# Masks from the first landing on, 14 pieces of block 1 ahead of the first fill, and layer 0 by pairs: a three-pass graph attention kernel on one core

## The reference

```python
def gat(h, mask, u, v, values):            # one pass
    e = leaky_relu(u[:, None] + v[None, :], 0.2)
    att = softmax(where(mask, e, -9e15), axis=1)
    return elu(att @ values)
# layer 0: values = entity_embs, then x = layernorm(x + elu(att @ entity_embs + x))
# layers 1, 2: h = 0.2 * x + 0.8 * gat(h, ...);  concat(x, h1, h2) @ mlp_w + mlp_b, residual, layernorm
```

## Time and profile before

| | us |
|---|---|
| median of 3 runs | 3445.28 (3441.72 to 3446.64) |
| the profiled execution | 3447.01 |
| its span in the trace | 3445.2 |

### The profile page before, as it was taken

How to read it: one execution, slowest core, us unless ns; L and a number is a source line. 1 busy time by engine, 2 the same in 40 slices (tenths; PEclk the granted TensorE clock), 3 DMA queues, 4 the chain that set the end, 5 groups by cost and what they waited for, 6 DMA issues and landing times. The chain is left out here.

```text
span 3445.2 us, 56585 instructions
## 1 busy us (share of the span) xinstructions
PE 3096.8 (90%) x21977; PEld 1071.2 (31%) x21977; DVE 2865.5 (83%) x5292; ACT 2274.0 (66%) x3934; POOL 280.9 (8%) x330
## 2 busy tenths in 40 slices
PE   1479999999999999699999999997999999999998
PEld 0123333333333333233333333332333333333333
DVE  5468888888888876699999999997888788888886
ACT  0247776666766767477777777784666666666665
POOL 0000000000000000000000000001112112211211
PEclk9989999999999999899999999998999999999999
DMA  8999999999999981221312222214667766766764
GB/s 242 287 346 342 342 338 338 335 341 333 342 341 332 342 259 55 86 86 64 112 71 105 79 96 87 88 62 135 166 158 166 188 155 161 178 167 163 170 150 80
DMA packets 441759, 679.29 MB, mean 197 GB/s; under 512 B 297474, under 2 KB 318082, under 8 KB 416914
## 3 DMA queue, kind: packets, MB, share of 16 engines
q1 hardware_dynamic: 409458, 564.40, 51.2%
q0 software_dynamic: 32032, 111.27, 16.2%
HBM read 430.10 MB, written 77.69 MB: 147 GB/s over the span
## 5 line engine op out<-in xcount | busy, mean ns | idle before, releaser
L1235 DVE SCALAR_TENSOR_TENSOR eps<-ua,v8col,cb 128x512 f32<-128x512 f32 x2800 | 1963.9, 753 | 294.5 <-ACT prob L630 218.4
L630 ACT ACTIVATE prob<-eps,v2col 128x512 f32<-128x512 f32 x2392 | 1526.2, 689 | 599.1 <-PE eps L810 588.9
L851 PE MATMUL acc<-prob,feat 128*64 128x512 f32 x4784 | 1216.5, 605 | 6.4 <-ACT acc_s L638 6.4
L810 PE MATMUL eps<-nt,nbig 128*64 128x512 fp8e4 (+2 forms) x6642 | 997.5, 385 | 150.7 <-DVE eps L1235 146.5
L810 PEld LDWEIGHTS eps<-nt,nbig 128*64 128x64 bf16 (+2 forms) x6642 | 327.7, 103 | 1032.0 <-DVE eps L1235 687.7
L851 PEld LDWEIGHTS acc<-prob,feat 128*64 128x64 f32 x4784 | 305.9, 137 | 381.7 <-issue 208.0
L1065 DVE TENSOR_SCALAR mi<-stage 128x1024 uint8<-128x1024 int32 x512 | 351.7, 688 | 66.4 <-DMA stage<-in_adj_dram 66.0
L630 ACT ACTIVATE mi<-eps,v2col 128x512 f32<-128x512 f32 x344 | 219.5, 687 | 102.0 <-PE eps L810 100.3
L630 ACT ACTIVATE stage<-eps,v2col 128x512 f32<-128x512 f32 x336 | 214.6, 687 | 95.1 <-PE eps L810 93.4
L860 PE MATMUL den<-prob,ones 128*32 128x512 f32 x2048 | 275.5, 610 | 0.0
L1074 DVE TENSOR_SCALAR edges<-nt 128x2048 int32<-128x2048 int32 x192 | 234.0, 1219 | 29.7 <-PE misc L821 15.2
(11 more groups left out here) (175 smaller groups left out, 1810.4 us busy)
## 6 DMA issues: line engine op xcount, KB each, us to landing
stage<-in_adj_dram SPq DMA_DIRECT2D x512, 512.0 KB, 6.8
nt<-nt_d SPq DMA_DIRECT2D x128, 1024.0 KB, 6.1
nt_d<-nt SPq DMA_DIRECT2D x64, 1024.0 KB, 7.1
prob<-prob POOLq DMA_DIRECT2D x64, 512.0 KB, 5.8
mi<-mi POOLq DMA_DIRECT2D x64, 512.0 KB, 6.4
stage<-stage POOLq DMA_DIRECT2D x64, 512.0 KB, 6.6
ub<-u_d SPq DMA_DIRECT2D x48, 256.0 KB, 5.2
xy_d<-xin POOLq DMA_DIRECT2D x32, 256.0 KB, 3.3
```

The source lines that it names most:

```text
L630: nc.scalar.activation(weights(l, b, j), eps[:, j % ES, :], ACT.Exp, bias=v2col[:, j:j + 1]).then_inc(s_p, 1)
L810: mm = nc.tensor.matmul(et[c:c + cols, :], nbig[:, c:c + cols], edge, start=False, stop=True, skip_group_check=True, tile_position=(0, c))
L851: mm = nc.tensor.matmul(acc[h:h + C, :], feat[:, l % 2, j, 0:C], weights(l, b, j), start=(k == 0), stop=(k == NT // 2 - 1))
L1235: dv.scalar_tensor_tensor(eps[:, j % ES, :], ua[:, par, :], v8col[:, j:j + 1], cb[:, par, :], ALU.add, ALU.max).then_inc(s_fill, 1)
```

## The change

- SP issues the first adjacency loads (now four) ahead of the weights, and x after unit 7. VectorE makes masks 0 to 3 first of all.
- `node_products` is split into the product and the sum (`node_sums`), and masks stand between these, `bounds`, `levels`, the edges and the head of block 0.
- `PRO`, the number of units ahead of the first fill, goes from 32 to 46, so block 0's loop makes 38 units instead of 52. `units_at` of the other blocks is as before.
- Four stage buffers instead of five (`SS`), six mask buffers instead of eight (`MR`).
- Layer 0 issues its mains by pairs after every second mask, two pairs behind, and its denominators two quads at a time, after the step t with t % 8 = 3; masks are 64 columns wide.
- `prob` has 12 slots instead of 8. In layer 2 the ring of 24 slots is the same size, with `mi` and `stage` holding 4 and 8 of them instead of 8 and 8.

```diff
-MR = 8
-PRO = UNITS
+MR = 6
+PRO = UNITS + 14
+X_AT = 7
+UB_AT = UNITS + 3
-SS = 5
+SS = 4
-GROUP = (QUAD, 2, 2)
-LAG = (1, 2, 2)
+PAIRLAG = 2
-TS = 2 * QUAD
-SLOTS = (TS, TS, 3 * TS)
+LAST_RING = 6
+TS = 3 * QUAD
-MASK_COLS = (32, 64, 64)
+HALF = 64
@@ sync
+            for h in range(SS):
+                adj_load(h)
             sp.wait_ge(s_zero, 4)
...
-            for h in range(SS):
-                adj_load(h)
-            sp.dma_start(feat[:, 1, :, 0:C], x.rearrange("(t p) c -> p t c", p=P)).then_inc(s_x0, 16)
             for h in range(PRO):
                 unit(h)
+                if h == X_AT:
+                    sp.dma_start(feat[:, 1, :, 0:C], x.rearrange("(t p) c -> p t c", p=P)).then_inc(s_x0, 16)
+                if h == UB_AT:
+                    sp.wait_ge(s_ust, 16)
+                    ub_load(0, 0, 0)
@@ scalar, probs
-                if l < 2 and j % GROUP[l] == 0 and not (l == 0 and b == 0 and j < TS):
-                    act.wait_ge(s_main, summed(l, b, j - TS + GROUP[l] - 1))
+                if l < 2 and tile(l, b, j) >= TS and j % 2 == 0:
+
+                    old, i = divmod(tile(l, b, j) - TS, NT)
+                    ol, ob = divmod(old, NB)
+                    if ol == 1:
+                        act.wait_ge(s_main, pairs(ol, ob, i // 2 + 1))
+                    else:
+                        act.wait_ge(s_den, dens(ol, ob, i // DEN + 1))
@@ tensor
-                n = GROUP[l]
-                first = j // n * n - 1
+                first = j // 2 * 2 - 1
...
-                return P if any(first <= t < first + n for t in whole) else MASK_COLS[l]
+                return P if any(first <= t < first + 2 for t in whole) else HALF
...
+            def two_quads(l, b, g):
+                denominators(l, b, 2 * g)
+                denominators(l, b, 2 * g + 1).then_inc(s_den, 1)
...
-                        if t % GROUP[l] == GROUP[l] - 1:
-                            k = t // GROUP[l] - LAG[l]
+                        if t % 2 == 1:
+                            k = t // 2 - PAIRLAG
                             if k >= 0:
-                                sums(l, b, k)
+                                main(l, b, k).then_inc(s_main, 1)
                             elif tail:
-                                sums(l, b - 1, NT // GROUP[l] + k)
+                                main(l, b - 1, NT // 2 + k).then_inc(s_main, 1)
...
+                        if l == 0 and t % DEN == DLAG:
+                            g = t // DEN - 1
+                            if g >= 0:
+                                two_quads(l, b, g)
+                            elif tail:
+                                two_quads(l, b - 1, NT // DEN + g)
@@ vector
+            for h in range(SS):
+                make_mask(h)
             dve.wait_ge(s_w, 16 * 14)
...
+                    masks(SS, 8)
                     dve.wait_ge(s_w0e, 1)
                     dve.wait_ge(s_feat0, 16)
                     node_products(0)
+                    masks(8, 10)
+                    node_sums(0)
+                    masks(10, 12)
                     bounds(0)
-                    for h in range(SS):
-                        make_mask(h)
+                    masks(12, 14)
                     levels(0)
+                    masks(14, 18)
                     dve.wait_ge(s_x0, 16)
                     node_products(1)
+                    masks(18, 20)
+                    node_sums(1)
                     dv.memset(feat[:, 1, :, C - 1:C], 1.0).then_inc(s_one, 1)
-                    for h in range(SS, PRO):
-                        make_mask(h)
-                        if h in (MU + 6, 2 * MU + 6):
-                            make_edges(0, 0, h // MU - 1)
+                    masks(20, 24)
+                    make_edges(0, 0, 0)
+                    masks(24, 28)
+                    make_edges(0, 0, 1)
+                    masks(28, UNITS + 6)
+                    make_edges(0, 0, 2)
+                    masks(UNITS + 6, UNITS + 9)
+                    make_edges(0, 0, 3)
+                    masks(UNITS + 9, UNITS + 12)
+                    head(0, 0, 0, 0)
+                    head(0, 0, 0, 1)
+                    head(0, 0, 0, 2)
+                    masks(UNITS + 12, PRO)
+                    add_u(0, 0, 0)
```

More of the change, by code:

```diff
@@ L318, in places @@
         def places(b, j):
-            q, o = divmod((b * NT + j) % SLOTS[2], TS)
-            return (prob[:, :, :], more, rest)[q], o
+            n = (b * NT + j) // QUAD % LAST_RING
+            buf = (prob[:, :, :], prob[:, :, :], prob[:, :, :], as_probs(mi[:, 0:QUAD, :]),
+                   as_probs(stage[:, :, :]), as_probs(stage[:, :, :]))[n]
+            return buf, (0, QUAD, 2 * QUAD, 0, 0, QUAD)[n] + j % QUAD
         def weights(l, b, j):
             if l < 2:
-                return prob[:, j % SLOTS[l], :]
+                return prob[:, tile(l, b, j) % TS, :]
             buf, o = places(b, j)
@@ L347, in den_blocks, with pairs, dens @@
             return b if l == 0 else (l - 1) * NB + b
[L349 to L357, removed]
+        def pairs(l, b, n):
+            return (l * NB + b) * (NT // 2) + n
+        def dens(l, b, n):
+            return den_blocks(l, b) * (NT // DEN) + n
         def started(l, b, j, on_act):
@@ L491, in body @@
                     if l == 0:
+                        ub_at = min((t for t in units_at(b) if t >= 10), default=NT)
                         for t, hs_ in sorted(units_at(b).items()):
-                            if t >= 10 and t < 12:
+                            if t == ub_at:
                                 ub_load(l, b + 1, 1 - par)
@@ L498, in body @@
                             store(NB * MV - 1)
-                        if head and not any(t in (10, 11) for t in units_at(b)):
+                        if head and ub_at == NT:
                             ub_load(l, b + 1, 1 - par)
@@ L633, in sums_out @@
             def sums_out(l, b, par):
[L634 to L637, removed]
+                act.wait_ge(s_main, pairs(l, b, NT // 2))
                 nc.scalar.activation(acc_s[:, :], acc[:, :], ACT.Copy).then_inc(s_acce, 1)
             def denominators_out(l, b):
[L641 to L644, removed]
+                act.wait_ge(s_den, dens(l, b, NT // DEN))
                 nc.scalar.activation(den_s[:, :], den[:, :], ACT.Copy).then_inc(s_dene, 1)
@@ L862, in denominators @@
                 return mm
[L864 to L871, removed]
             def eight_probs(b, g):
@@ L1013, in _ @@
                 blocks(body)
[L1014 to L1019, removed]
+                for k in range(NT // 2 - PAIRLAG, NT // 2):
+                    main(l, NB - 1, k).then_inc(s_main, 1)
+                if l == 0:
+                    two_quads(l, NB - 1, NT // DEN - 1)
+                for g in DEN_ORDER if l == 2 else ():
+                    if DEN * (g + 1) + (ADDLAG if g in ADDED else DLAG) >= NT:
+                        eight_probs(NB - 1, g)
                 for t in range(NT):
@@ L1033, in step, with make_mask @@
                 dve.wait_ge(seq, n)
+            def make_mask(h):
+                b, u = divmod(h, UNITS)
+                n, c = h // MU, u % 2
+                dve.wait_ge(s_stage[h % SS], 16 * (h // SS + 1))
+                if u % MU == 0 and n >= 2:
+                    s, count = landed(0, (n - 2) // MV, (n - 2) % MV)
+                    dve.wait_ge(s, count)
+                out = mi[:, h // 2 % MR, c * CW:(c + 1) * CW].rearrange("q (g p o) -> q g o p", p=P, o=2)
+                src = stage[:, h % SS, :].rearrange("q (g o p) -> q g o p", p=P, o=2)
+                dv.tensor_scalar(out, src, 0, ONE8, ALU.is_le, ALU.mult).then_inc(s_mask, 1)
+            for h in range(SS):
+                make_mask(h)
             dve.wait_ge(s_w, 16 * 14)
@@ L1053, in _ @@
             ins.then_inc(s_q0, 1)
[L1055 to L1065, removed]
             def make_edges(l, b, m):
@@ L1290, in levels, with masks @@
                 step(dv.tensor_scalar(v2col[:, :], v, ALPHA, None, ALU.mult), s_oneh, l + 1)
+            def masks(first, end):
+                for h in range(first, end):
+                    make_mask(h)
             for l in range(NLAYER):
@@ L1315, in _ @@
                     levels(l)
-                for m in range(2, MV):
-                    make_edges(l, 0, m)
-                for part in range(3):
-                    head(l, 0, 0, part)
-                add_u(l, 0, 0)
+                    for m in range(2, MV):
+                        make_edges(l, 0, m)
+                    for part in range(3):
+                        head(l, 0, 0, part)
+                    add_u(l, 0, 0)
                 def body(b, par, head_, tail_):
```

47 lines of the change are left out of this document (23 added, 24 removed).

## The result

The changed kernel takes 3388.63 us (median, 3387.21 to 3391.65) against 3444.11 for the kernel before in the same runs: a ratio of 0.9839 (95% interval 0.9825 to 0.9852), 55.5 us less. The forecast was 3387.

A forecast was written before the change was run, and what follows sets the result against it. Block 0 was taken as DMA-bound, the stretch ahead as bound by order, then DMA, and steady layer 0 as not DMA-bound. 3447.0 - 43 - 15 = 3389; less 1.7, 3387 us; range 3352 to 3425.

The forecast's parts named there:

- Start and block 0: Launch to block 1's first fill: block 1 starts at 199 instead of 242.3, -43 us, bounds -31 and -53.
- Mask 20: Preparation on VectorE with masks between its steps: 31 + 27 + 8 + 5 = 71 us at mask 20.
- The first fill: End of the start, after mask 45: at 119 us against 127.5, bounds 113 and 127.
- the head's chain: Before the first fill: 25 us of transposes, edge counts and row maxima, forecast to lie covered under landings.
- no gap over 6 us in the masks: Sign in VectorE's masks from 25 us on: no gap over 6 us.
- Pairs: Layer 0's steady blocks: -1.1 us a block from column-width changes; no gain from stalls, bounds -2 and +1.
- the width term: TensorE in layer 0: column-width changes cost 5.1 us a block in quads, 4.0 in pairs.
- rival B: Layer 0: pairs take away stalls too, another -2.5 us a block, 38 us, to 3349; chance 0.12.
- Four stage buffers: Layer 0's load loop: median 8.1 us fits 9.6, so +0.1 us a block, bounds 0 and +2.5.
- Rival D: Layer 0: four stage buffers make the landing loop the bound; at 10.2 us, blocks 81.6, total 3474; chance 0.08.
- VectorE's waits for landings: Sign on VectorE: waits for landings small after block 0.
- Rival A: Steady layer 0 paced by VectorE and ScalarE, not TensorE's passes; only -43 stays, 3402 us; chance 0.18.

The follow-up runs named there:

- e3: Kernel before with four stage buffers instead of five, nothing else changed: 3462.7 us, ratio 1.0052.
- e1: Changed kernel with layer 0's sums back in quads and masks 32 wide: 3435.6 us, ratio 0.9974.
- e2: Kernel before with only layer 0's mains in pairs and masks 64 wide, denominators one quad at a time: 3407.2 us, ratio 0.989.
- e7: Kernel before with the new start and layer 0 pairs, denominators one quad at a time, five stage and eight mask buffers kept: 3371.6 us, ratio 0.9791.
- e5: Changed kernel with layer 0's denominators one quad at a time after every fourth mask, four stage buffers kept: 3414.4 us.
- e10: Changed kernel with five stage buffers instead of four and four mask buffers instead of six: 3372.3 us.
- e9: Changed kernel with layer 0's masks cut into four 32-column matmuls again, mains staying in pairs: 3423.0 us.
- the early head: e7 with quarter 3's edges made after mask 36 instead of 40 and block 0's head after mask 39 instead of 43: 3372.5 us.
- the lead of 48: e7 with masks kept 48 instead of 52 units ahead, so block 0 makes 34 units: 3373.6 us.

## Why the prediction was right, and where it was not

To compare its terms I divide TensorE's rows into passes and stalls: the distance from each pass's start to the next, the least distance in any of the nine kernels of the same kind of neighbours (with the width of the pass before them) taken as its price, the rest as stall. The numbers are means of the 12 blocks between the copies of blocks 1 and 13, in us. Other ways to part the kinds move the border between the two by about 1 us, and the differences between kernels by about half a us. Beside them stand TensorE's waits for fills in 500 to 800 us.

```
one block, us             passes   stalls   weight loads'   matmuls'
                                            wait in 300     wait in 300
before                     72.6      4.2        30.0          10.2
four buffers only (e3)     72.6      5.8        36.7          16.0
quads back (e1)            72.6      6.4        38.3          15.7
pairs only (e2)            72.1      2.2        41.9           4.2
pairs, new start (e7)      72.1      2.2        43.1           3.4
single quads (e5)          72.1      5.0        55.0          12.6
the changed kernel         70.4      5.3        44.4          11.9
five buffers (e10)         70.6      3.8        39.2           8.2
32-wide masks (e9)         75.2      2.2        29.7           6.4
```

*The sum.* In the profiled runs 43 + 15 + 0 = 58 us were forecast and 55.4 measured: 34.5 for the start and block 0, 18.2 for the rest of layer 0, and 2.7 in layers 1 and 2, to which I had given nothing. The start fell short by 8.5 us, and the other two made up for 6 of them.

*Start and block 0: -43 forecast, -34.5 measured* (242.26 to 207.74), within the bounds. Mask 20 was put at 71 and stands at 69.59. The first fill was put at 119 and stands at 124.53, and the rows show two places where it was lost. In SP's timeline of the changed kernel a transpose issue holds the queue 6 us, behind a store and the ub load, and mask 40 comes after 7 us of waiting:

```profile
99.67 0.58 SPq L465 DMA_DIRECT2D nt_d<-nt  x1
100.29 0.59 SPq L420 DMA_DIRECT2D ub<-u_d  x1
100.93 0.94 SPq L396 DMA_DIRECT2D stage<-in_adj_dram  x2
101.91 6.13 SPq L448 DMA_TRANSPOSE nt<-mi  x1
```

In the kernel before, the ub load was issued after the last unit; I had not counted it among what the moved step brings into the queue. That it is what lengthens the hold is not shown: without it a transpose issue behind a store held SP 4.1 to 4.9 us there. And the head's chain was taken as fully covered, where masks 44 and 45 stand behind it in VectorE's order, at 121.12. Block 0 took 83.2 us against 80. That it was bound by landings is borne out by the early head and by the lead of 48. One of my signs failed here, "no gap over 6 us in the masks", by that wait of 6.98.

*Pairs: -1.1 forecast for width changes, nothing for stalls.* As a price the width term was in the right direction: the changed kernel's passes are about 2 us shorter than before (72.6 to 70.4), and the 5.2 us forecast for 32-wide masks are 75.2 - 70.4 = 4.8 there. It was wrong for the run with pairs alone, where I had forecast 1.0 us more and the passes are 0.5 shorter. But as a gain in time the width is worth a third, since a stall shrinks where a pass grows: 1.7 of 4.8 us reached the block.

The step that failed is that pairs were given nothing for stalls. What pays is the grouping: alone on the kernel before, pairs take 2.5 us off a block, 0.5 of it in passes and 2.0 in stalls (4.2 to 2.2). Between the runs with quads back and with 32-wide masks the passes even grow by 2.6 and the stalls shrink by 4.2. Nearly all stalls before stand between two mask passes in a row (3.8 of 4.2 us, 1.9 with pairs), where TensorE waits for a fill. That this comes from ScalarE being fed after every second tile instead of in fours fits the rows (ScalarE's wait for scores falls from 71.4 to 62.3 us in 300, and the mains' weight loads, which waited 20.3 for probabilities, are no longer in the list), but no run tests that link by itself.

This was rival B, whose extra 2.5 a block measured 2.0 alone. I spoke against it with the waits of layer 2, and that reading failed: the weight loads' wait for fills went up with pairs (30.0 to 41.9 us in 300) while the block got shorter. In the table the weight loads' wait doesn't go with the stalls, and the matmuls' own wait does.

*Four stage buffers: +0.1 forecast, +1.6 measured* in the one clean comparison (76.80 to 78.40 in quads). With two quads of denominators it is 1.3 (74.43 to 75.75, with two mask buffers more), with single quads 2.8 (74.27 to 77.07, with other numbers of mask buffers and slots too). The step that failed is the comparison of a median loop of 8.1 us with 9.6. It left out the wait of a load behind a transpose that SP is issuing (line L446 before: 2.3 us median, 5.3 at most for an issue), and it set a median against a limit that every unit has to meet. With a mask of 0.7 us a load has to land 8.9 us after the mask that frees its buffer. In the kernel before, where 11.3 were allowed, 101 of the 363 loads from 300 to 1170 us took longer than 8.9, and 15 longer than 11.3; in the changed kernel 65 of 367 took longer than 8.9, at most 11.1. Rival D named this mechanism and was put off by the median. VectorE's waits for landings, which my signs wanted small after block 0, were 55.2 us from 300 to 1230.

Two sizes were wrong the opposite way, over 2 us a block for pairs and 1.3 to 1.6 for buffers, and so 75.8 a block was forecast and 75.75 measured. That this came out is luck, and so is the total, where the late start was made up by terms that the forecast didn't have.

*Rival A* is refuted as it was put: VectorE's work per block is nearly the same before, in the changed kernel and with pairs alone (65.25, 65.15 and 65.54 us), and the blocks are 76.80, 75.75 and 74.29. What is right in it is that TensorE's passes alone don't set the pace either. The Trainium skill, "Perfetto Trace Analysis", section "Identifying the Most-Contended Engine", says that matmul busy time is not a good measure and that weight loads' busy share is to be used. The first is borne out only in a small way: the stalls come to 4.2 us in a block in which the rows leave TensorE idle for 3.2 (73.58 busy of 76.80). By the second TensorE had room with a third of its time in weight loads, and still the block changed with the order of TensorE's work.

## What to carry to other kernels

When two edits are costed against the same slack, run each alone: here one gave back over half of what the other brought, and only the sum looked right. Before a buffer is taken from a load loop, count in the trace how many loads land later than the shorter loop allows, with the time that they wait for the issuing queue; the median says nothing on that. Cut the work between two masks into small groups: here that saved four times as much in stalls (2.0 us a block) as in passes (0.5), and it paid even where it cost changes of array width. To see whether TensorE is held up, read the waits of its matmuls and not those of its weight loads.

## What the runs showed of the hardware

The price of a change of column width adds up in TensorE's rows (4.8 us for 5.2 worked out from single gaps), yet two thirds of it vanished in stalls. And the wait for landings depended on how TensorE's work was grouped: with four buffers 15.1 us in 300 with two quads of denominators, 25.2 with single quads, for the same DMAs in the same order. I have no run that shows why; the share of loads that land over 8.9 us after their mask is about the same in both (65 of 367 and 57 of 362).
